# First attention as probabilities times context, turned by DMA; expert blocks whose last products follow two blocks behind

## The reference, cut to what matters

```python
# layer 0 attention: 16 query heads, 4 key/value heads, head size 128
q = rmsnorm(layernorm(x) @ Wq + bq)
k = rmsnorm(ctx @ Wk + bk)
v = ctx @ Wv + bv
probs = softmax(q @ k.T / sqrt(128) + mask)
x = x + (probs @ v) @ Wo
# layer 0 ffn: router, top 6 of 32 experts and a shared expert
d = ragged_dot(silu(g) * u, w_down, group_sizes)
x = x + sum(d * weights) + shared
# layer 1 attention: 16 heads of size 16 on the same context, then an int4 ffn
```

## Time and profile before

| what | value |
|---|---|
| median of 3 runs | 5748.51 us (5746.48 to 5749.6) |
| the profiled execution's own time | 5724.92 us |
| its span | 5723.2 us |
| busy in the span | PE 81%, PE's weight loads 64%, DVE 69%, ACT 49%, POOL 31% |

### The profile page before, as it was taken

How to read it: one execution, slowest core, us unless ns; L and a number is a source line. 1 busy time by engine, 2 the same in 40 slices (tenths; PEclk the granted TensorE clock), 3 DMA queues, 4 the chain that set the end, 5 groups by cost and what they waited for, 6 DMA issues and landing times. The chain is left out here.

```text
span 5723.2 us, 119501 instructions
## 1 busy us (share of the span) xinstructions
PE 4635.3 (81%) x39954; PEld 3681.8 (64%) x39955; DVE 3950.1 (69%) x7266; ACT 2792.3 (49%) x5207; POOL 1760.5 (31%) x2107
## 2 busy tenths in 40 slices
PE   4679999999999999999997407743888888888865
PEld 2447777777777777777776306632666666666654
DVE  4757777777777777777764633356777777777767
ACT  2335555555555555555543133321666666666643
POOL 2544444444444444444430163344000000000003
PEclk9789999999999999999998659975999998989976
DMA  5222112112212211221204274444333333333320
GB/s 191 89 62 57 38 49 57 50 42 52 52 41 51 57 48 44 52 52 40 52 27 122 76 217 124 124 128 116 93 86 87 83 87 81 90 78 89 89 52 24
DMA packets 395261, 436.41 MB, mean 76 GB/s; under 512 B 184225, under 2 KB 352801, under 8 KB 384526
## 3 DMA queue, kind: packets, MB, share of 16 engines
q1 hardware_dynamic: 366558, 388.13, 26.2%
q0 software_dynamic: 9216, 22.03, 1.2%
q10 hardware_dynamic: 19008, 19.40, 1.0%
HBM read 187.81 MB, written 144.83 MB: 58 GB/s over the span
## 5 line engine op out<-in xcount | busy, mean ns | idle before, releaser
L1804 DVE TENSOR_SCALAR_CACHE_REDUCE b_pr<-b_ps 112x1500 f32<-112x1500 f32 x256 | 439.3, 1716 | 279.4 <-PE b_ps L1879 279.1
L701 POOL TENSOR_TENSOR a_ksq<-a_kb 125x512 f32<-125x512 f32 x384 | 399.0, 1039 | 708.8 <-DVE a_kb L651 708.5
L616 ACT ACTIVATE a_pTh<-a_pt 125x448 f16<-125x448 f32 x768 | 402.7, 543 | 326.0 <-PE a_pt L775 321.4
L1761 ACT ACTIVATE b_pTh<-b_pt 125x448 f16<-125x448 f32 x768 | 392.7, 542 | 340.4 <-PE b_pt L1892 336.3
L673 DVE CUSTOM_DVE_ANT_0 a_pr<-a_ps,a_mask 112x1500 f32<-112x1500 f32 x256 | 439.7, 1718 | 164.7 <-PE a_ps L112 162.8
L110 PE MATMUL a_po<-a_vh,a_pTh 125*112 125x128 f16 x3072 | 549.5, 220 | 3.7 <-DVE a_pTl L689 3.1
L112 PE MATMUL a_po<-a_vh,a_pTl 125*112 125x128 f16 x3072 | 547.4, 219 | 0.0
L111 PE MATMUL a_po<-a_vl,a_pTh 125*112 125x128 f16 x3072 | 547.0, 219 | 0.0
L1811 DVE TENSOR_TENSOR b_pTl<-b_pt,b_pTh 125x448 f16<-125x448 f32 x768 | 454.0, 616 | 72.6 <-ACT b_pTh L1761 69.2
L1892 PE MATMUL b_pt<-ident,b_pr 112*125 112x112 f32 x3072 | 474.4, 294 | 32.0 <-DVE b_pTl L1811 26.9
L1997 POOL PARTITION_ALL_REDUCE f_ma<-f_mx x1 | 0.4, 374 | 1588.3 <-DVE f_mx L2057 1588.3
(11 more groups left out here) (376 smaller groups left out, 13470.8 us busy)
## 6 DMA issues: line engine op xcount, KB each, us to landing
b_ks<-b_kn SPq DMA_DIRECT2D x384, 187.5 KB, 4.4
scratch_cT<-a_cT SPq DMA_DIRECT2D x128, 375.0 KB, 3.1
b_cT<-scratch_cT SPq DMA_DIRECT2D x32, 1500.0 KB, 6.9
a_ctx<-ctx SPq DMA_DIRECT2D x32, 1440.0 KB
scratch_yd<-e_y SPq DMA_DIRECT2D x88, 256.0 KB, 2.1
...
```

Source lines behind the costliest of these rows:

```text
L616: nc.scalar.activation(pTh[:, r % 2, 4 * third:4 * third + 4].rearrange("p k c -> p (k c)"), ps_t[n % 2][0:KP, 0:4 * RP], ACT.Copy).then_i ...
L701: nc.gpsimd.tensor_tensor(ksq[:, kt % 2], kb[0:KP, kt % 4], kb[0:KP, kt % 4], ALU.mult).then_inc(s["k_squared"], 1)
L1804: nc.vector.tensor_scalar(pr[:, n % 2].rearrange("p (a k) -> p a k", k=500), ps_s[0:RP, :, 0:500], -1.0, None, ALU.mult, ALU.min, accum_ou ...
```

## The change

Values are no longer made for each context row. The probabilities are multiplied with the context itself (P, 24 steps a batch: 4 key heads, two halves of 128 features, three thirds of 12 products with 224 columns), and the small result is multiplied with Wv (O, 6 products of 224 columns a head). C, U, T and V go. The probabilities, already divided by their sum, are split before they are turned: H on ScalarE into `a_ph`, L on VectorE into `a_pl`, each 112 by 1500. SyncE turns both with DMA transposes (turn), and so it turns the split context (D on ScalarE and GpSimd, `a_ch` and `a_cl`, in quarters) into `a_cT` (turn_ctx), now padded to 128 rows a tile. G splits the first product's result, Z adds the value bias and splits the output, already turned, which phase m reads as it is; turn_o and split_o go. On GpSimd, q squares one key tile and N normalises two at a time. D belongs to the batch two ahead, K, R, Q, q and N to the next. The loop body (`rounds`) holds six batches. In phase e the down products, the copy of their result and its store follow two blocks behind. The second attention reads the padded context.

```diff
+LAG = 2
...
-        S0 T23< K0 V21< C1 V22< V23< T0 U0 K1 T1 T2 C2 S1 R0 U1 V0 V1 K2 C3 T3 T4 U2 R1 S2 V2 C4 T5 K3 V3 R2 V4
+        S4 R4 P5 K8 S5 K9 P6 R5 S6 P7 P8 P9 P10 O3< R6 K10 O0 K11 R7 S7 P11 R8 P12 P13 R9 P14 P15 P16 O1 R10
...
+        cx = a.sb("a_ctx", [KP, 2, 3, H])
+        ch = a.sb("a_ch", [128, RING, KT, H], F16)
+        cl = a.sb("a_cl", [128, RING, KT, H], F16)
+        cT = a.sb("a_cT", [128, 2, KT, KC, 128], F16)
...
+            def load_ctx(tile, p):
+
+                G = tile[0]
+                wait(sp, s["c_lo"], 4 * G + p - 1)
+                passed(sp, sp_gate)
+                src = io.ctx[ds(G, 1), :, :].rearrange("a (p k) d -> (a p) k d", k=KT)[:, 3 * p:3 * p + 3]
+                sp.dma_start(cx[0:120, p % 2], src[0:120]).then_inc(ctx_in[p % 2], 16)
+                sp.dma_start(cx[120:KP, p % 2], src[120:KP]).then_inc(ctx_in[p % 2], 16)
...
+            def turn_ctx(tile, half):
+
+                G = tile[0]
+                k, _ = of_three(tile)
+                part = slice(HT * half, HT * half + HT)
+                wait(sp, s["work_done"], NW * (G - 1) + AT["K", HT * half + HT - 1] + 1)
+                passed(sp, sp_gate)
+                wait(sp, kept[half], 16 * G)
+                passed(sp, sp_gate)
+                sp.wait_ge(s["c_lo"], 4 * G + 2 * half + 2)
+                passed(sp, sp_gate)
+                for n, c in enumerate((ch, cl)):
+                    sp.dma_start_transpose(out=cT[:, n, part].rearrange("p k c q -> p (k c) q"),
+                                           in_=c[:, k, part].rearrange("q k d -> q (k d)")).then_inc(c_turned[half], 16)
...
+            def keep_ctx(tile, half):
...
+                sp.wait_ge(c_turned[half], 32 * G + 32)
+                passed(sp, sp_gate)
+                sp.dma_start(io.cT[ds(G, 1), :, :, part].rearrange("a p n k c q -> p (a n) (k c q)"),
+                             cT[:, :, part].rearrange("p n k c q -> p n (k c q)")).then_inc(kept[half], 16)
...
+            def turn(tile, r):
+
+                G, h, k = tile[0], r // 2, r % 2
+                wait(sp, s["mix_done"], NKV * G + h - 1)
+                passed(sp, sp_gate)
+                for n, (p, pT, ready) in enumerate(((ph, pTh, "p_hi"), (pl, pTl, "p_lo"))):
+                    sp.wait_ge(s[ready], NR * G + r + 1)
+                    passed(sp, sp_gate)
+                    sp.dma_start_transpose(out=pT[:, h % 2, :, k], in_=p[:, k].rearrange("q k c -> q (k c)"))\
+                        .then_inc(turned[n][k], 16)
...
+                if kind == "D":
+                    ring, _ = of_three(batch)
+                    half = 2 * G + n // 2
+                    act.wait_ge(ctx_in[n % 2], 32 * half + 32)
+
+                    wait(act, s["mix_done"], NKV * (G - RING) + NKV)
+                    nc.scalar.activation(ch[0:KP, ring, 3 * n:3 * n + 3], cx[:, n % 2], ACT.Copy).then_inc(s["c_hi"], 1)
...
+                elif kind == "H":
+                    act.wait_ge(s["inv_ready"], NR * b + n + 1)
+
+                    wait(act, turned[0][n % 2], 16 * (NKV * b + n // 2))
+                    nc.scalar.activation(ph[:, n % 2, :, 0:KP], pr[:, n % 2].rearrange("p (k c) -> p k c", c=KP),
+                                         ACT.Copy, scale=inv[:, par, n:n + 1]).then_inc(s["p_hi"], 1)
+                elif kind == "G":
+                    act.wait_ge(s["mix_done"], NKV * b + n + 1)
+
+                    wait(act, s["values_done"], NKV * b + n - 1)
+                    nc.scalar.activation(ah[:, n % 2], ps_a[n % 2][:], ACT.Copy, scale=1 / PS).then_inc(s["mix_hi"], 1)
...
+                elif kind == "L":
+                    dve.wait_ge(s["p_hi"], NR * b + n + 1)
+
+                    wait(dve, turned[1][n % 2], 16 * (NKV * b + n // 2))
+                    nc.vector.scalar_tensor_tensor(pl[:, n % 2, :, 0:KP],
+                                                   pr[:, n % 2].rearrange("p (k c) -> p k c", c=KP),
+                                                   inv[:, par, n:n + 1], ph[:, n % 2, :, 0:KP], ALU.mult,
+                                                   ALU.subtract).then_inc(s["p_lo"], 1)
...
+                    nc.gpsimd.tensor_tensor(cl[0:KP, ring, 3 * n:3 * n + 3], cx[:, n % 2],
+                                            ch[0:KP, ring, 3 * n:3 * n + 3], ALU.subtract).then_inc(s["c_lo"], 1)
...
+                    nc.gpsimd.tensor_tensor(rk[:, 1], rk[:, 0], g.mhalf[0:KP, 0:2 * NKV], ALU.pow).then_inc(pool_own, 1)
...
+                elif kind == "P":
+                    h, c, third = n // 6, n // 3 % 2, n % 3
+                    ring, _ = of_three(batch)
+                    if n % 6 == 0:
+
+                        wait(pe, s["mix_lo"], NKV * b + h - 1)
+                        for t in turned:
+                            for k in range(2):
+                                pe.wait_ge(t[k], 16 * (NKV * b + h) + 16)
+                    for kt in range(4 * third, 4 * third + 4):
+                        feat = slice(c * 128, c * 128 + 128)
+                        last = three_products(nc, ps_a[h % 2][:, c], ch[0:KP, ring, kt, feat], cl[0:KP, ring, kt, feat],
+                                              pTh[0:KP, h % 2, kt].rearrange("p r q -> p (r q)"),
+                                              pTl[0:KP, h % 2, kt].rearrange("p r q -> p (r q)"),
+                                              start=(kt == 0), stop=(kt == KT - 1))
+                    if n % 6 == 5:
...
+                    cols = slice(n * HD, n * HD + HD)
+                    for c in range(KC):
+                        last = three_products(nc, ps_o[:], wv[:, c, 0, cols], wv[:, c, 1, cols], ah[:, n % 2, c],
+                                              al[:, n % 2, c], start=(c == 0), stop=(c == KC - 1))
+                    last.then_inc(s["values_done"], 1)
...
-            pipeline(act, NT, [(split_o, 1), (take_logits, -2), (split_x, -1)])
+            pipeline(act, NT, [(take_logits, -2), (split_x, -1)])
...
-            pipeline(dve, NT, [(normalise, -1), (split_o, 1), (split_x, -1), (residual, 0)])
+            pipeline(dve, NT, [(normalise, -1), (split_x, -1), (residual, 0)])
...
-            pipeline(pe, NT, [(turn_o, 1), (route, -2), (project, 0), (turn_x, -1)])
+            pipeline(pe, NT, [(route, -2), (project, 0), (turn_x, -1)])
...
-            pipeline(sp, NS, [(load, 2), (store, -1)])
+            pipeline(sp, NS, [(load, 2), (store, -LAG)])
...
-            pipeline(dve, NS, [(product, 0), (take, -1)])
+            pipeline(dve, NS, [(product, 0), (take, -LAG)])
...
-                    g.be[0:1, ds(GB * i, GB + 1)], [mybir.EngineType.PE], min_val=0, max_val=NX - 1)
+                    g.be[0:1, ds(GB * i, GB + LAG)], [mybir.EngineType.PE], min_val=0, max_val=NX - 1)
                 for n in range(GB):
                     t = GB * i + n
-                    up(t, n % 2, GB // 2 * i + n // 2, held[n + 1])
-                    if n or follows:
-                        down(t - 1, 1 - n % 2, held[n])
-                return held[GB]
+                    up(t, n % 2, GB // 2 * i + n // 2, held[n + LAG])
+                    if n >= LAG or follows:
+                        down(t - LAG, n % 2, held[n])
+                return held[GB:]
 
...
-        cT = a.sb("b_cT", [128, 2, 2, KC, SE], F16)
+        cT = a.sb("b_cT", [128, 2, 2, KT, KC, 128], F16)
...
-                    keys = slice(GK * j, GK * j + GK)
+                    keys = slice(4 * j, 4 * j + 4)
```

More of the change, by code:

```diff
@@ L459, in batches, with moved, rounds, turn @@
         turn((g_, g_ % 2, g_ // 2))
+RING = 3
+ROUND = 2 * RING
+def moved(tile, d):
+    n, k, i = tile
+    return n + d, (k + d) % ROUND, i + (k + d) // ROUND
+def rounds(eng, steps, attend, work):
+    def turn(batch):
+        for kind, n, off in steps:
+            lead = {"D": 2, "K": 1, "R": 1, "q": 1, "N": 1, "Q": 1}.get(kind, 0)
+            at = moved(batch, off + lead)
+            if exists(at, B):
+                (work if lead else attend)(kind, n, at)
+    count = (B - 4) // ROUND
+    for b in (-2, -1, 0):
+        turn((b, b % ROUND, b // ROUND))
+    with eng.Fori(0, count) as i:
+        for k in range(1, ROUND + 1):
+            turn((ROUND * i + k, k % ROUND, i + k // ROUND))
+    for b in range(ROUND * count + 1, B + 1):
+        turn((b, b % ROUND, b // ROUND))
+def of_two(tile):
+    n, k, i = tile
+    return k % 2, RING * i + k // 2
+def of_three(tile):
+    n, k, i = tile
+    return k % RING, 2 * i + k // RING
 def attn0_phase(nc, g, io):
@@ L575, in _ @@
+            for p in range(2):
+                load_ctx(at(2), p)
+            count = (B - 4) // ROUND
+            step(at(0))
+            with sp.Fori(0, count) as i:
+                for k in range(1, ROUND + 1):
+                    step((ROUND * i + k, k % ROUND, i + k // ROUND))
+            for b in range(ROUND * count + 1, B):
+                step(at(b))
+            store(NT - 1)
+            sp.wait_ge(stored, 16 * NT)
```

(18 more changed lines are left out.)

478 lines of the change are left out of this document (221 added, 257 removed).

## The result

The changed kernel takes 5305.45 us (median of four runs, 5289.14 to 5310.41) against 5749.05 us for the kernel before on the same chip: a ratio of 0.9224, 95% interval 0.9204 to 0.9244, 444 us less. The forecast was 5260 us, 489 less. The profiled execution took 5289.14 us.

A forecast was written before the change was run, and what follows sets the result against it. TensorE was taken as the bound, 97.3% busy in the first attention. 5724.9 - 400 (first attention with start) - 46 (mixing) - 42 (experts) = 5237, plus 23.6 from profiled execution to median: 5260 us, range 5180 to 5370.

The forecast's parts named there:

- New products, 0.095 us each: First attention, TensorE: 288 P products of 224 columns a batch at 0.095 us, 27.4 us; bounds 0.056 and 0.109 each.
- Idle time, 4.0 us a batch: First attention, TensorE: present idle 2.2 us plus 1.8 for VectorE's tighter schedule and waits, giving 69.7 us a batch.
- None of them becomes the bound: First attention: VectorE, ScalarE and GpSimd all stay under TensorE's 65.7 us a batch.
- L, 1.68 us; squares and scalings, 1.04: First attention: VectorE's L 1.68 us each, 13.4 a batch; GpSimd's 24 squares and scalings 1.04 us each.
- Start, +22: Before the first score: clearing `a_ch` and `a_cl`, chained quarters and a transpose add 22 us; bounds 10 and 45.
- DMA: First attention's queue: 344 KB transposes hold SyncE 1.63 us and land after 4.3; engines 62% busy, all hidden.
- Rival two: SyncE is held by each transpose out of SBUF until it lands and becomes the bound: about 6010 us; chance 0.13.
- rival one: First attention: turned rows land late, over 6.6 us; at 9 us the total is 5455; chance 0.14 with rival three.
- Rival three: First attention: VectorE binds if L costs twice its row, about 75 us a batch, 5425; chance 0.14 with rival one.
- Mixing, -46: Phase m: a tile falls from 9.9 to 7.0 us, 46 us saved; bounds 0 and 59.
- Experts, -42: Phase e: down products' 44.0 us of waits go, loads add 2, 42 us saved; bounds 0 (loads gate) and 50.
- 23.6 us from the profiled execution to the median: Whole kernel: the median before is 23.6 us above the profiled execution's own time, added to 5237 to give 5260.

The follow-up runs named there:

- e10: Changed kernel with two instead of three products per tile of probabilities times context, the one with the context's low part left out; ratio 0.9239 to the kernel before.
- e3: Changed kernel with the loop of the first attention written out, so no engine jumps back there; ratio 0.904 to the kernel before.
- e5: Changed kernel with L's subtraction left out and an extra one-input VectorE operation of 900 elements ahead of each L; ratio 0.9062 to the kernel before.
- e9: Changed kernel with the store of two batches' context rows in two parts, heads 0 to 11 ahead of 12 to 15; ratio 0.917 to the kernel before.
- e6: Changed kernel with each transpose of a high part of the probabilities issued twice, first into a spare tile; ratio 0.9242 to the kernel before.
- e4: Changed kernel where L reads only the exponentials, without the subtraction, leaving out the probabilities' low part; ratio 0.8927 to the kernel before.
- e1b: Changed kernel with the expert phase's down products one block behind instead of two, in the other buffer; ratio 0.9292 to the kernel before.
- e2: Kernel before with only the expert phase's down products moved to two blocks behind; ratio 0.979 to the kernel before.
- e7: Changed kernel with 128 small semaphore instructions ahead of the second attention in TensorE's program; ratio 0.9244 to the kernel before.

## Why the prediction came out as it did

- **New products, 0.095 us each.** Right: 0.095. TensorE's work in a batch: from 2242 to 2597 us, five batches behind the loop, it is busy 332.7 us, 66.5 a batch; forecast 65.7.
- **Idle time, 4.0 us a batch.** This step failed. Behind the loop it is 4.5, and there a batch takes 71.1; in the loop it is about 8 (447 / 6 - 66.5), and a batch averages 73.8 instead of 69.7. So 31 batches gave 299 us, not 426. "None of them becomes the bound" was the wrong sentence: in e10 TensorE has 9.0 us a batch less to do and gains nothing, and its longest wait is for the chain of K, square, sum, power, scaling and R. Three things were missing, and since their waits overlap, their sizes don't add up: the jumps, where each engine stands at its own time and a lower clock follows (58 us, e3); the hold of GpSimd by L (e5, where each hold is shorter, takes 86 us less; what no hold at all would give was not run); the store of two batches that holds ScalarE (28 us, e9).
- **L, 1.68 us; squares and scalings, 1.04.** 1.88, 1.25 and 1.43. GpSimd is busy 969.6 / 1400 x 73.8 = 51 us a batch, forecast 38 to 43. H (1.55), Q (1.22) and the power (1.66) came inside their bounds.
- **Start, +22.** It was +3. The two clearings took 7.78 us each (forecast 9.4), but GpSimd idled 39.9 us there in the kernel before, so most of it was probably covered; I had put it all on the path, and no run here leaves the clearings out. The first attention with its start gave 320 us where the sum had 400.
- **DMA.** Hold 1.36 us (forecast 1.63, bounds 1.24 and 4.3), landing 3.1 (forecast 4.3), share 0.68 (forecast 0.62). The Trainium skill's sequencer time (DMA: Bandwidth & Descriptors, the table of sequencer times) gave the estimate of 2.2 us: too long by 0.8. Rival two is refuted by the hold, rival one by the landing and by e6. Rival three named the right operation with the wrong size: L took 1.88 us, not twice 1.68. It was dear through GpSimd, which the rival lacked; whether VectorE's own time counted beside it (in the 79 us between e4 and e5), no run decides.
- **Mixing, -46.** Measured -53, 6.9 us a tile (forecast 7.0), and no wait for its load.
- **Experts, -42.** -43 us by e1b and its neighbours, -44 by e2: right, and the load's gating never showed. The -56 of the two profiles is more than the lag: the other kernels with it take 326 to 335 us, not 320.8.
- **Second attention, 0.** -34 in this pair of profiles, by the holes at TensorE's jumps (8.2 us before, 5.2 after), which no row of the change points to.
- **23.6 us from the profiled execution to the median.** The trace of before had the short gap (208.5 us) that one job showed and the others not; the job of e1b and e5 to e7 suggests that the offset was this. After the change it is 16.3 us.

That the total came out nearer (45 us) than its main term is partly luck. The first attention with its start fell 80 us short; 34 us of the second attention and 21 more in mixing and experts came back, and the gap took 25 again. Neither the 34 nor the 25 is explained.
